# The state scan of a macaron block: the drive product written over b in PSUM, and eight products moved to GpSimd

## The chip, the cores and the metric

One core of one Trainium2 chip. The metric is the device time of one execution in microseconds (us). The kernel before takes 3356.19 us, the median of 3 runs (3346.16 to 3364.49). Engines by their names in the profile: PE is TensorE (PEld its weight loads), DVE is VectorE, ACT is ScalarE, POOL is GpSimd, SP is SyncE.

## The reference

The input x is 8 sequences of 256 tokens of width 128. Three residual parts follow each other: x + 0.5 F(norm x), then x + M(norm x), then x + 0.5 F(norm x) again, with F a stack of 6 layers of windowed attention and a gated feed-forward, 16 heads of 64. The change lies in M alone, a selective state space layer with 16 states:

```python
A = -jnp.exp(A_log)
dt = jax.nn.softplus(u @ W_dt + b_dt)
Bt = u @ W_B
Ct = u @ W_C
def step(h, inp):
    dt_t, B_t, C_t, u_t = inp
    dA = jnp.exp(dt_t[..., None] * A)
    h = dA * h + (dt_t * u_t)[..., None] * B_t[:, None, :]
    y = jnp.einsum('bdn,bn->bd', h, C_t)
    return (h, y)
...
x_ssm = _selective_scan(x_conv, A_log, D_skip, W_dt, b_dt, W_B, W_C)   # ys + u * D_skip
v = _silu(x_norm @ v1_w + v1_b)
return x_ssm * v @ w2_w + w2_b
```

## The kernel before

Channels lie on the 128 partitions, tokens along the free dimension. The 2048 tokens are 4 chunks of 512 columns (2 sequences), so every tile of M is 128 x 512 f32. PSUM has eight banks of that size: seven `general` banks and `sums`.

M runs between the two stacks of attention layers. For each chunk `c` it is prepared in 24 small stages (`("prepare", c, i)`: layer norms, projections, convolution, step size), then scanned in 16 states (`("state", c, i)`), then finished in 3 stages (`("finish", c, i)`: skip term and gate, output projection, residual). That makes 64 states, numbered `at` = 16 c + i. One state is, on each engine:

- PE: `tensor_part` spreads row i of B over all partitions into `b_bank[at % 2]` (L1354, one fp32r matmul) and row i of C into `c_bank[at % 2]` (the same line), then adds the product of three states earlier into the accumulator bank (`pe_added`, L1406, an fp32 matmul with the identity that the profile records as two).
- ACT: `act_decay` makes exp(dt A) two states ahead (L1548); a copy brings c from PSUM to SBUF as `c_kept` (L1568).
- DVE: `dve_drive` multiplies `m_dtu` (dt times u) by b out of PSUM into an SBUF tile `drive[at % 3]` (L1417), one state ahead; `tensor_tensor_scan` runs h = decay h + drive over the 512 columns (L1433), both inputs and the output in SBUF.
- POOL: `gpsimd_part` multiplies h by c into `hc` (L1622).

Two more products belong to the change: at prepare stage 23 DVE makes `m_dtu = m_dt * m_u` (L1537), and at finish stage 0 DVE adds the skip term to the accumulated y (L1439) and multiplies it by the gate (L1443). Each occurs once per chunk.

The order is fixed when the program is built. `parts_beside` gives each engine a list of parts: three states in each of the last six steps of the first attention stack (18 states), and the other 46 states behind that stack. After each state at most two side stages (prepare, finish, start) follow. A side stage stands after the state of its own slot on DVE and POOL, one state later on ACT and two states later on PE (`SIDE_LATE`). Every engine works through its list in order, and waits on semaphores.

The waits around b: PE may fill `b_bank[at % 2]` again when `m_drive` says that drive `at - 2` is done. PE may fill `c_bank` when `c_kept` of `at - 2` is done. DVE issues drive `at + 1` ahead of scan `at`.

Of the kernel before, what the change touches and what calls it, by code (L numbers as in the profile page):

```python
# [28 lines left out]
STATES = 16  # L29
# [349 lines left out]
def macaron_kernel(nc, x_in, consts_in, vec_in, mvec_in, wqkv_in, wo_in, w1_in, w2_in,  # L379
                   mw_in, wb_in, out):  # L380
    ctx = ExitStack()
    with ctx:
# [73 lines left out]
        m_xn, m_centered, m_square, m_turned = ([prep_tiles[c % 3][j] for c in range(CHUNKS)] for j in range(4))  # L456
        m_z, m_e, m_ln, m_corr = m_xn, m_centered, m_square, m_turned
        m_u, m_dt, m_dtu, m_gate = ([(v_tiles[4:8] + tiles)[4 * c + j] for c in range(CHUNKS)] for j in range(4))
        decay, hc, c_kept, hstate, drive, m_y = tiles[12:16], tiles[16:20], tiles[20:23], tiles[23:26], tiles[26:29], v_tiles[0:2]
        bc = [wqkv_hi[:, 2:, :].rearrange("p a c -> p (a c)")[:, c * COLS:(c + 1) * COLS] for c in range(CHUNKS)]  # L460
        b_bank, c_bank, acc_bank = general[2:4], general[4:6], [general[6], sums]

# [878 lines left out]
        def tensor_part(e, w, kind, c, i):  # L1341
            if kind == "state":
                at = c * STATES + i
                if at == 0:

                    for sem, value in BANKS.before_states:
                        w.wait_ge(S[sem], value)
                    w.wait_ge(S["sums_kept"], ITEMS)
                    w.wait_ge(S["m_sel"], 1)
                w.wait_ge(S["m_bc_parts"], c + 1)  # L1350
                for row, g, done, read in ((i, b_bank, "m_b", "m_drive"), (STATES + i, c_bank, "m_c", "m_c_kept")):
                    w.wait_ge(S[read], at - 1)
                    sel = row_sel[:, row:row + 1].broadcast_to([P, P])
                    e.matmul(g[at % 2][:, :], sel, bc[c], start=True, stop=True).then_inc(S[done], 1)  # L1354
                if at >= 3:
                    pe_added(e, w, at - 3)
            elif kind == "added":
                pe_added(e, w, c * STATES + i)
            elif kind == "finish":
                if i == 1:  # L1360
                    w.wait_ge(S["m_gated"], c + 1)
                    g = pe_bank(w, ("m_last", c))
                    e.matmul(g[:, :], mw[:, 3, :], m_y[c % 2], start=True, stop=True).then_inc(S["m_last"], 1)
            elif kind == "start":
                if i == 0:
                    pe_enter(e, w, 1, 0, 0)
                elif i == 2:
                    pe_enter(e, w, 1, 0, 1)
            elif kind == "out":
                w.wait_ge(S["half_added"], CHUNKS + i + 1)  # L1370
                g = pe_bank(w, ("out", i))
                for j in range(4):
                    turn = e.transpose(g[:, j * P:(j + 1) * P], x[:, (4 * i + j) * P:(4 * i + j + 1) * P], ident)
                turn.then_inc(S["out_turned"], 1)
            elif kind == "prepare":
                if i == 0:
                    w.wait_ge(S["half_added"], c + 1)
                    g = pe_bank(w, ("m_center", c, 0))
                    e.matmul(g[:, :], center, chunk(c), start=True, stop=True).then_inc(S["m_centered0"], 1)
                elif i == 7:  # L1380
                    w.wait_ge(S["m_scaled0"], c + 1)
                    g = pe_bank(w, ("m_center", c, 1))
                    e.matmul(g[:, :], center, m_xn[c], start=True, stop=True).then_inc(S["m_centered1"], 1)
                elif i in (2, 9):
                    w.wait_ge(S[f"m_squared{i // 7}"], c + 1)
                    g = pe_bank(w, ("m_var", c, i // 7))
                    e.matmul(g[:, :], mean, m_square[c], start=True, stop=True).then_inc(S[f"m_var{i // 7}"], 1)
                elif i == 14:
                    w.wait_ge(S["m_affine"], c + 1)
                    w.wait_ge(S["m_loaded"], 48)  # L1390
                    for name, m in (("m_x1", 0), ("m_v1", 1)):
                        g = pe_bank(w, (name, c))
                        e.matmul(g[:, :], mw[:, m, :], m_xn[c], start=True, stop=True).then_inc(S[name], 1)
                elif i == 18:
                    w.wait_ge(S["m_u"], c + 1)
                    g = pe_bank(w, ("m_dt", c))
                    e.matmul(g[:, :], mw[:, 2, :], m_u[c], start=True, stop=True).then_inc(S["m_dt"], 1)
                    g = pe_bank(w, ("m_bc", c))
                    e.matmul(g[:, :], wbc, m_u[c], start=True, stop=True).then_inc(S["m_bc"], 1)
# [12 lines left out]
        def dve_drive(e, w, at):  # L1412
            c = at // STATES
            w.wait_ge(S["m_b"], at + 1)
            w.wait_ge(S["m_drive_in"], c + 1)
            w.wait_ge(S["m_scan"], at - 2)
            e.tensor_tensor(drive[at % 3], m_dtu[c], b_bank[at % 2][:, :], ALU.mult).then_inc(S["m_drive"], 1)  # L1417

        def vector_part(e, w, kind, c, i):
            r = c % 2  # L1420
            if kind == "state":
                at = c * STATES + i
                if at == 0:
                    scan_tiles_free(w)
                    w.wait_ge(S["m_ahead_zeroed"], 1)
                    dve_drive(e, w, 0)
                if at + 1 < CHUNKS * STATES:
                    dve_drive(e, w, at + 1)
                w.wait_ge(S["m_drive"], at + 1)
                w.wait_ge(S["m_decay"], at + 1)  # L1430
                w.wait_ge(S["m_hc"], at - 2)

                e.tensor_tensor_scan(hstate[at % 3], decay[at % 4], drive[at % 3], 0.0, ALU.mult, ALU.add).then_inc(S["m_scan"], 1)  # L1433
            elif kind == "finish":
                if i == 0:
                    w.wait_ge(S["m_acc"], (c + 1) * STATES)
                    w.wait_ge(S["m_last"], c - 1)
                    w.wait_ge(S["m_step"], 2)
                    e.scalar_tensor_tensor(out=m_y[r], in0=m_u[c], scalar=mcol(M_D), in1=acc_bank[r][:, :], op0=ALU.mult, op1=ALU.add)\  # L1439
                        .then_inc(S["m_skip"], 1)  # L1440
                    w.wait_ge(S["m_skip"], c + 1)
                    w.wait_ge(S["m_gate"], c + 1)
                    e.tensor_tensor(m_y[r], m_y[r], m_gate[c], ALU.mult).then_inc(S["m_gated"], 1)  # L1443
                elif i == 2:
                    w.wait_ge(S["m_last"], c + 1)
                    e.scalar_tensor_tensor(out=chunk(c), in0=general_of(("m_last", c))[:, :], scalar=mcol(M_W2B), in1=chunk(c),
                                           op0=ALU.add, op1=ALU.add).then_inc(S["m_done"], 1)
            elif kind == "start":
                if i == 3:
                    dve_enter(e, w, 1, 0, 1)  # L1450
                elif i == 5:
                    dve_enter(e, w, 1, 0, 2)
                elif i == 7:
                    dve_first_splits(e, w, 1)
            elif kind == "half":

                w.wait_ge(S[f"base{i}_loaded"], 16 * (c + 1))
                w.wait_ge(S["ffn_added"], c * ITEMS + ITEMS - CHUNKS + i + 1)
                e.scalar_tensor_tensor(out=chunk(i), in0=chunk(i), scalar=0.5, in1=base[i], op0=ALU.mult, op1=ALU.add)\
                    .then_inc(S["half_added"], 1)  # L1460
            elif kind == "out":
                w.wait_ge(S["out_turned"], i + 1)

                w.wait_ge(S["valued"], (2 * ITEMS - 1) * GROUPS)
                e.tensor_copy(stage_out[:, 4 * i:4 * i + 4, :], general_of(("out", i)).rearrange("p (h d) -> p h d", d=P))\
                    .then_inc(S["out_kept"], 1)
            elif kind == "prepare":
                dve_prepare(e, w, c, i)

        def dve_prepare(e, w, c, i):  # L1470
# [57 lines left out]
            elif i == 23:  # L1528
# [4 lines left out]
                e.tensor_tensor(m_ln[c], m_ln[c], m_corr[c], ALU.subtract).then_inc(S["m_ln1"], 1)  # L1533
                w.wait_ge(S["m_ln1"], c + 1)
                e.scalar_tensor_tensor(out=m_dt[c], in0=m_z[c], scalar=0.0, in1=m_ln[c], op0=ALU.max, op1=ALU.add).then_inc(S["m_step"], 1)
                w.wait_ge(S["m_step"], c + 1)
                e.tensor_tensor(m_dtu[c], m_dt[c], m_u[c], ALU.mult).then_inc(S["m_drive_in"], 1)  # L1537

        def vector_scan(e, w):
            for what in SCAN_ORDER["DVE"]:  # L1540
# [66 lines left out]
        def gpsimd_part(e, w, kind, c, i):  # L1607
# [15 lines left out]
            elif kind == "start":  # L1623
                if i == 1:
                    pool_enter(e, w, 1, 0, 0)
                elif i == 5:
                    pool_enter(e, w, 1, 0, 2)
            elif kind == "prepare":
                if i in (1, 8):
                    w.wait_ge(S[f"m_kept{i // 7}"], c + 1)  # L1630
# [4 lines left out]
                elif i == 13:  # L1635
                    w.wait_ge(S["m_back1"], c + 1)
                    e.tensor_tensor(m_centered[c], m_centered[c], m_square[c], ALU.mult).then_inc(S["m_scaled1"], 1)
                    w.wait_ge(S["m_scaled1"], c + 1)
                    e.tensor_scalar(m_xn[c], m_centered[c], mcol(M_G), mcol(M_B), ALU.mult, ALU.add).then_inc(S["m_affine"], 1)

        def gpsimd_scan(e, w):
            for what in SCAN_ORDER["POOL"]:
# [94 lines left out]
```

## Time and profile before

| | before |
|---|---|
| median of 3 runs | 3356.19 us |
| profiled execution, its own time | 3364.97 us |
| its span, first to last instruction | 3363.2 us |
| busy: PE / DVE / POOL / ACT | 86% / 87% / 72% / 61% |
| granted TensorE clock, mean | 0.946 |
| M's scan, first drive to end of last scan | 1584.46 to 1793.14 us, 208.7 us |

In the page's forty slices of the span (84 us each) the scan fills slices 19 to 21, between the two attention stacks; there PE and POOL are less busy than elsewhere and DVE is not. In a group of instructions the columns are: line, engine, operation, output<-inputs, shape, count, then busy us and mean ns of one, then the idle time of the engine just ahead of the group and what ended it. In a timeline the columns are the start in us, the duration in us, engine, line and operation; brackets hold the idle time before it. An SBUF tile is named by the buffer in which it lies: the `hstate` and `drive` tiles are `v_buf`; the decay tiles are `q_ring` or `k_ring`; a bank of PSUM is `general` or `sums`.

### The profile page before, as it was taken

Reading aid. Unit: us, or ns where it says so; the run is one execution under the profiler, and the core shown is the slowest. Engines: PE = TensorE matmul, PEld = TensorE weight load, DVE = VectorE, ACT = ScalarE, POOL = GpSimd, SP = SyncE. Lnnn points to the kernel's source line nnn. Section 1 sums busy time; section 2 is a strip of 40 time slices with the busy share of each in tenths; the row PEclk is TensorE's granted clock in tenths of the full one; section 3 lists DMA queues with packets and bytes.
Section 4 is the critical chain, followed back from the end, with each engine's and each line's share of the span. In section 5 each row is a group of like instructions: output and inputs, shape, how many; then the busy total and the mean of one; then the engine's idle time right before and its main releaser. Section 6 shows DMA issues by size and latency. Waiting matters only on the chain. (4 is left out here: it accounts for less than half of the span.)

```text
span 3363.2 us, 132089 instructions
## 1 busy us (share of the span) xinstructions
PE 2891.1 (86%) x57914; PEld 1829.9 (54%) x57914; DVE 2933.3 (87%) x4224; ACT 2059.8 (61%) x3820; POOL 2423.5 (72%) x1679
## 2 busy tenths in 40 slices
PE   5689988988999989897677788999998989998987
PEld 3455555655666655553233455555565555555553
DVE  6789989999999988986898789889899989898984
ACT  3466666666676666665663566666566666566663
POOL 3678787787787787874464678778787787787773
PEclk8899999999999999998897899999999999999998
DMA  5233333333333333320002233333343333342330
GB/s 136 65 80 77 82 91 74 84 92 71 84 92 73 89 85 72 88 65 28 10 4 59 68 81 78 75 93 77 73 101 73 86 90 71 82 94 65 88 74 15
DMA packets 114726, 250.85 MB, mean 75 GB/s; under 512 B 27244, under 2 KB 60648, under 8 KB 114152
## 3 DMA queue, kind: packets, MB, share of 16 engines
q1 hardware_dynamic: 114152, 242.40, 30.5%
q8 instruction: 457, 7.49, 1.0%
q14 instruction: 117, 0.96, 0.1%
HBM read 37.82 MB, written 3.15 MB: 12 GB/s over the span
## 5 line engine op out<-in xcount | busy, mean ns | idle before, releaser
L1096 ACT ACTIVATE squares<-general 128x512 f32<-128x512 f32 x768 | 453.7, 597 | 716.8 <-PE general L661 707.8
L1290 POOL TENSOR_TENSOR probs<-probs,row_sum 128x1024 f32<-128x1024 f32 x192 | 365.4, 1903 | 442.4 <-DVE row_sum L968 442.3
L1270 POOL TENSOR_TENSOR q_ring<-q_ring,partner 128x512 f32<-128x512 f32 x384 | 491.0, 1279 | 203.9 <-DMA partner<-sines 203.3
L881 DVE TENSOR_TENSOR sines<-general,layer_tables 128x512 f32<-128x512 f32 x768 | 515.8, 672 | 85.3 <-ACT squares L1096 81.8
L1270 POOL TENSOR_TENSOR k_ring<-k_ring,partner 128x512 f32<-128x512 f32 x384 | 490.9, 1278 | 0.0
L695 PE MATMUL general<-probs_t,v_buf 32*64 32x64 f32 x24576 | 339.0, 234 | 153.8 <-issue 85.1
L659 PE MATMUL general<-xs_hi,wqkv_lo 128*128 128x512 f32 x768 | 454.2, 591 | 18.5 <-DVE xs_lo L908 8.0
L695 PEld LDWEIGHTS general<-probs_t,v_buf 32*64 32x64 f32 x24576 | 304.0, 134 | 246.1 <-issue 237.5
L1284 POOL TENSOR_TENSOR probs<-probs,q_scale 128x1024 f32<-128x1024 f32 x192 | 365.4, 1903 | 15.1
L722 PE MATMUL general<-k_ring,q_ring 64*32 64x64 f32 (+1 forms) x24576 | 295.3, 223 | 92.5 <-issue 53.1
L671 PE MATMUL general<-att,wo 128*128 128x512 f32 x768 | 366.2, 621 | 4.6 <-ACT att L1166 4.2
L1276 POOL TENSOR_TENSOR probs<-probs,row_max 128x1024 f32<-128x1024 f32 x192 | 366.7, 1910 | 0.0
L722 PEld LDWEIGHTS general<-k_ring,q_ring 64*32 64x32 f32 x24576 | 261.1, 105 | 126.8 <-issue 109.4
L661 PE MATMUL general<-xs_hi,wqkv_hi 128*128 128x512 f32 x768 | 313.1, 408 | 2.3 <-issue 2.2
L660 PE MATMUL general<-xs_lo,wqkv_hi 128*128 128x512 f32 x768 | 313.1, 408 | 1.9 <-issue 1.9
L659 PEld LDWEIGHTS general<-xs_hi,wqkv_lo 128*128 128x128 f32 x768 | 152.1, 198 | 267.9 <-issue 235.5
L1166 ACT ACTIVATE att<-general 128x256 f32<-128x256 f32 x768 | 231.4, 388 | 93.0 <-PE general L695 92.6
L902 DVE STREAM_TRANSPOSE v_buf<-general 128x512 f32<-128x512 f32 x384 | 264.8, 690 | 25.4 <-PE general L754 25.2
L733 PE MATMUL sums<-squares,consts 128*32 128x512 f32 x1536 | 249.0, 612 | 38.8 <-ACT squares L1096 36.5
L963 DVE TENSOR_REDUCE row_sum<-probs 128x16 f32<-128x1024 f32 x192 | 230.2, 1199 | 52.2 <-ACT probs L1173 51.8
L951 DVE TENSOR_TENSOR probs<-general,k_inv 128x512 f32<-128x512 f32 x384 | 244.8, 677 | 29.7 <-PE general L722 27.7
L752 PE MATMUL general<-xs_hi,wqkv_lo 128*128 128x256 f32 x768 | 258.7, 337 | 3.5 <-issue 3.5
(233 smaller groups left out, 6369.9 us busy)
## 6 DMA issues: line engine op xcount, KB each, us to landing
partner<-sines SPq DMA_DIRECT2D x1536, 128.0 KB, 2.3
wqkv_raw<-in_wqkv SPq DMA_DIRECT2D x80, 208.0 KB, 2.7
wo<-in_wo SPq DMA_DIRECT2D x12, 512.0 KB, 5.1
w<-in_w SPq DMA_DIRECT2D x12, 341.0 KB, 3.2
base_dram<-x SPq DMA_DIRECT2D x8, 256.0 KB, 2.4
att<-in_wqkv SPq DMA_DIRECT2D x2, 1024.0 KB, 6.7
sines<-base_dram SPq DMA_DIRECT2D x8, 256.0 KB, 3.9
w<-in_w SPq DMA_DIRECT2D x12, 128.0 KB
```

The costliest lines, as they stand in the source:

```text
L659: e.matmul(g[:, :], wqkv_lo[:, p, cut], xs_hi[:, r, :], start=True, stop=False)
L660: e.matmul(g[:, :], wqkv_hi[:, p, cut], xs_lo[:, r, :], start=False, stop=False)
L661: e.matmul(g[:, :], wqkv_hi[:, p, cut], xs_hi[:, r, :], start=False, stop=True)\
L671: done = e.matmul(g[:, :], wo[:, p, :], att[:, p, :], start=(p == OUT_PAIRS[i][0]), stop=(p == OUT_PAIRS[i][-1]))
L695: done = e.matmul(o, lhs, rhs, start=(kb == 0), stop=True, skip_group_check=True)
L722: done = e.matmul(o, qw, kw, start=False, stop=True, skip_group_check=True)
L881: e.tensor_tensor(by_seq(sines[:, i % 2, which, :]), g, both(layer_tables[:, 2 * which + 1, :]), ALU.mult).then_inc(S[f"sin_{side}"], 1)
L1096: e.activation(squares[:, (2 * p + which) % 4, :], general_of(("proj", k, n, p, which))[:, :], ACT.Square).then_inc(S[f"squared_{side}"], 1)
L1270: e.tensor_tensor(y, y, partner[:, i % 2, which, :], ALU.add).then_inc(S[f"rotated_{side}"], 1)
L1276: e.tensor_tensor(y, y, spread_keys(row_max[:, i % 2, :]), ALU.subtract).then_inc(S["max_off"], 1)
L1284: e.tensor_tensor(y, y, spread_keys(q_scale8[:, n % 2, group, :]), ALU.mult).then_inc(S["q_norms_off"], 1)
L1290: e.tensor_tensor(y, y, spread_keys(row_sum[:, i % 2, :]), ALU.mult).then_inc(S["probs_done"], 1)
```

## The change

The drive is written back over b, in the bank from which b is read, and the scan takes it from there; the three SBUF tiles for it are gone. The drive of a state is now issued just ahead of its own scan. PE may fill a bank of b again when the scan that read it is done. The `m_dtu` product and the gate product go from DVE to POOL, at the same slots.

```diff
-        decay, hc, c_kept, hstate, drive, m_y = ..., tiles[26:29], v_tiles[0:2]
+        decay, hc, c_kept, hstate, m_y = ..., v_tiles[0:2]
...
-                for row, g, done, read in ((i, b_bank, "m_b", "m_drive"), (STATES + i, c_bank, "m_c", "m_c_kept")):
+                for row, g, done, read in ((i, b_bank, "m_b", "m_scan"), (STATES + i, c_bank, "m_c", "m_c_kept")):
                     w.wait_ge(S[read], at - 1)
...
             w.wait_ge(S["m_b"], at + 1)
             w.wait_ge(S["m_drive_in"], c + 1)
-            w.wait_ge(S["m_scan"], at - 2)
-            e.tensor_tensor(drive[at % 3], m_dtu[c], b_bank[at % 2][:, :], ALU.mult).then_inc(S["m_drive"], 1)
+            b = b_bank[at % 2][:, :]
+            e.tensor_tensor(b, b, m_dtu[c], ALU.mult).then_inc(S["m_drive"], 1)
...
-                    dve_drive(e, w, 0)
-                if at + 1 < CHUNKS * STATES:
-                    dve_drive(e, w, at + 1)
+                dve_drive(e, w, at)
                 w.wait_ge(S["m_drive"], at + 1)
                 w.wait_ge(S["m_decay"], at + 1)
                 w.wait_ge(S["m_hc"], at - 2)
-                e.tensor_tensor_scan(hstate[at % 3], decay[at % 4], drive[at % 3], 0.0, ALU.mult, ALU.add).then_inc(S["m_scan"], 1)
+                e.tensor_tensor_scan(hstate[at % 3], decay[at % 4], b_bank[at % 2][:, :], 0.0, ALU.mult, ALU.add).then_inc(S["m_scan"], 1)
...   in vector_part, finish 0, and in dve_prepare, stage 23: removed; in gpsimd_part, the same stages: added
+            elif kind == "finish":
+                if i == 0:
+                    w.wait_ge(S["m_skip"], c + 1)
+                    w.wait_ge(S["m_gate"], c + 1)
+                    e.tensor_tensor(m_y[c % 2], m_y[c % 2], m_gate[c], ALU.mult).then_inc(S["m_gated"], 1)
...
+                elif i == 23:
+                    w.wait_ge(S["m_step"], c + 1)
+                    e.tensor_tensor(m_dtu[c], m_dt[c], m_u[c], ALU.mult).then_inc(S["m_drive_in"], 1)
```

## Rows read from the trace of the kernel before

**Rows 1.** Busy time by engine in the scan, granted clock, DMA share.
```profile
core 0: us, PE busy (x) PEld busy (x) DVE busy (x) ACT busy (x) POOL busy (x), PEclk, DMA share, GB/s
1584.40:1793.20 208.80, 147.09 (x317) 64.48 (x315) 194.71 (x208) 134.58 (x193) 110.40 (x78) 0.86 0.02 7
```

**Rows 2.** All waits of DVE in the scan: us in total, times, longest.
```profile
DVE v_buf L1417 <- PE general L1354: 9.8, 6, 2.6
DVE squares L1488 <- PE general L1387: 1.1, 1, 1.1
DVE partner L1502 <- PE general L1393: 1.1, 1, 1.1
DVE att L1485 <- PE general L1383: 0.3, 1, 0.3
DVE v_buf L1433 <- ACT q_ring L1548: 0.2, 1, 0.2
DVE att L1488 <- PE general L1387: 0.2, 1, 0.2
```

**Rows 3.** Groups of DVE instructions in the scan, by line and operands.
```profile
L1433 DVE TENSOR_TENSOR_SCAN v_buf<-k_ring,v_buf 128x512 f32<-128x512 f32 x32 | 51.3, 1602 | 0.0
L1433 DVE TENSOR_TENSOR_SCAN v_buf<-q_ring,v_buf 128x512 f32<-128x512 f32 x32 | 49.6, 1549 | 0.2 <-ACT q_ring L1548 0.2
L1417 DVE TENSOR_TENSOR v_buf<-q_ring,general 128x512 f32<-128x512 f32 x48 | 31.8, 662 | 3.6 <-PE general L1354 3.5
L1443 DVE TENSOR_TENSOR v_buf<-v_buf,k_ring 128x512 f32<-128x512 f32 x2 | 2.2, 1109 | 0.1
L1443 DVE TENSOR_TENSOR v_buf<-v_buf 128x512 f32<-128x512 f32 x1 | 1.6, 1576 | 0.0
L1537 DVE TENSOR_TENSOR q_ring<-k_ring,q_ring 128x512 f32<-128x512 f32 x3 | 2.5, 842 | 0.1
```

**Rows 4.** Minimum, median, maximum ns of L1417 (one input in PSUM) and L1433.
```profile
L1417 DVE TENSOR_TENSOR v_buf<-q_ring,general x48: 627/657/689, 1647.9 to 1789.5; 128x512 f32<-128x512 f32 x48
L1433 DVE TENSOR_TENSOR_SCAN v_buf<-q_ring,v_buf x32: 1209/1388/1989, 1586.0 to 1790.1; 128x512 f32<-128x512 f32 x32
```

**Rows 5.** Timeline of DVE and POOL in two states, 1652 to 1657.
```profile
1653.08 1.22 DVE L1433 TENSOR_TENSOR_SCAN v_buf<-q_ring,v_buf 128x512 f32<-128x512 f32 x1
1654.21 0.66 DVE L1417 TENSOR_TENSOR v_buf<-q_ring,general 128x512 f32<-128x512 f32 x1
1654.43 1.27 POOL L1622 TENSOR_TENSOR q_ring<-v_buf,k_ring 128x512 f32<-128x512 f32 x1 [3.20 <-DVE v_buf L1433]
1654.79 1.98 DVE L1433 TENSOR_TENSOR_SCAN v_buf<-k_ring,v_buf 128x512 f32<-128x512 f32 x1
1656.70 0.66 DVE L1417 TENSOR_TENSOR v_buf<-q_ring,general 128x512 f32<-128x512 f32 x1
```

**Rows 6.** Timeline of a DVE pair in which the second reads the first's output.
```profile
1674.92 0.69 DVE L1533 TENSOR_TENSOR att<-att 128x512 f32<-128x512 f32 x1
1675.65 0.69 DVE L1535 SCALAR_TENSOR_TENSOR k_ring<-att 128x512 f32<-128x512 f32 x1
```

**Rows 7.** ACT instructions that write PSUM, groups of 1560 to 1900.
```profile
L1148 ACT ACTIVATE general<-mask_bf 128x512 f32<-128x512 bf16 x7 | 3.9, 590 | 0.0
```

**Rows 8.** Timeline of PE, one state at the full clock, one at half.
```profile
1658.03 1.03 PE L1354 MATMUL general<-wqkv_hi,row_sel 128*128 128x512 f32 x2
1659.36 1.03 PE L1354 MATMUL general<-wqkv_hi,row_sel 128*128 128x512 f32 x2
...
1605.54 1.84 PE L1354 MATMUL general<-wqkv_hi,row_sel 128*128 128x512 f32 x2
1608.10 1.84 PE L1354 MATMUL general<-wqkv_hi,row_sel 128*128 128x512 f32 x2
```

**Rows 9.** Timeline of the end of the scan, from the last two products on POOL.
```profile
1791.95 1.19 DVE L1433 TENSOR_TENSOR_SCAN v_buf<-k_ring,v_buf 128x512 f32<-128x512 f32 x1
1792.16 2.04 POOL L1622 TENSOR_TENSOR q_ring<-v_buf 128x512 f32<-128x512 f32 x1 [1.21 <-DVE v_buf L1433]
1794.16 1.26 POOL L1622 TENSOR_TENSOR k_ring<-v_buf,q_ring 128x512 f32<-128x512 f32 x1
1798.68 0.69 DVE L1443 TENSOR_TENSOR v_buf<-v_buf,k_ring 128x512 f32<-128x512 f32 x1
1799.42 1.12 PE L1363 MATMUL general<-v_buf,wqkv_raw 128*128 128x512 f32 x2 [1.57 <-DVE v_buf L1443]
1800.59 0.75 DVE L1446 SCALAR_TENSOR_TENSOR x<-general,mvec,x 128x512 f32<-128x512 f32 x1 [1.22 <-PE general L1363]
```

More of the change, by code:

```diff
@@ L458, in macaron_kernel @@
         m_u, m_dt, m_dtu, m_gate = ([(v_tiles[4:8] + tiles)[4 * c + j] for c in range(CHUNKS)] for j in range(4))
-        decay, hc, c_kept, hstate, drive, m_y = tiles[12:16], tiles[16:20], tiles[20:23], tiles[23:26], tiles[26:29], v_tiles[0:2]
+        decay, hc, c_kept, hstate, m_y = tiles[12:16], tiles[16:20], tiles[20:23], tiles[23:26], v_tiles[0:2]
         bc = [wqkv_hi[:, 2:, :].rearrange("p a c -> p (a c)")[:, c * COLS:(c + 1) * COLS] for c in range(CHUNKS)]
@@ L1440, in vector_part @@
                         .then_inc(S["m_skip"], 1)
-                    w.wait_ge(S["m_skip"], c + 1)
-                    w.wait_ge(S["m_gate"], c + 1)
-                    e.tensor_tensor(m_y[r], m_y[r], m_gate[c], ALU.mult).then_inc(S["m_gated"], 1)
                 elif i == 2:
@@ L1535, in dve_prepare @@
                 e.scalar_tensor_tensor(out=m_dt[c], in0=m_z[c], scalar=0.0, in1=m_ln[c], op0=ALU.max, op1=ALU.add).then_inc(S["m_step"], 1)
-                w.wait_ge(S["m_step"], c + 1)
-                e.tensor_tensor(m_dtu[c], m_dt[c], m_u[c], ALU.mult).then_inc(S["m_drive_in"], 1)
         def vector_scan(e, w):
```

## The prediction, made before the changed kernel ran

> **What bounds the kernel now.** The page's forty slices come first: they show where M lies, and that the two attention stacks around it hold none of the changed instructions. Only the scan, 208.7 us, can gain or lose. The view of busy time by engine then shows DVE busy 194.7 of 208.8 us there, PE 147, ACT 135, POOL 110 [rows 1]. The list of DVE's waits adds the rest: 9.8 + 1.1 + 1.1 + 0.3 + 0.2 + 0.2 = 12.7 us of idle, 12.5 of it ended by PE [rows 2]. So DVE sets the pace and PE is next. The granted clock is 0.86; with two levels that means about 28% of the stretch at 1.2 GHz [rows 1]. A whole state of PE's own work (b, c, one addition) goes round in 1659.36 - 1658.03 = 1.33 us at 2.4 GHz and in 1608.10 - 1605.54 = 2.56 us at 1.2 GHz [rows 8].
>
> **The scan itself.** The groups give 32 scans of 1602 ns and 32 of 1549, a mean of 1.576 us [rows 3], but the shortest take 1.21 and the longest 1.99 [rows 4]. The timeline says why: a scan with POOL idle takes 1.22. The next is called at 1654.79 while POOL's product runs from 1654.43 to 1655.70, and ends at 1656.77, 1.07 us after POOL is done [rows 5]. The scan waits for POOL's instruction and then runs. The drive, issued in the middle of the same POOL instruction, takes 0.66, and all 48 of its group lie between 0.627 and 0.689 [rows 4]: a DVE instruction with one input in PSUM isn't held. In the change the scan has one SBUF input and one in PSUM, as the drive has. I take it as unheld: 1.21 us.
>
> **Part 1, the states.** Before, start to start: drive to scan 0.58 (1654.21 to 1654.79), scan to next drive its duration less 0.07 [rows 5]. Per state 0.58 + 1.576 - 0.07 = 2.09 us, and 64 of them 133.5 us. After, the scan needs the drive just issued. A dependent pair on DVE starts 1675.65 - 1674.92 = 0.73 us apart for a first of 0.69, that is 0.04 after its end, where independent ones overlap by 0.07 [rows 6, 5]. The drive of 0.66 gives 0.70 to the scan, the scan 1.21 - 0.07 = 1.14. Per state 1.84 us, 64 of them 117.8: **15.7 us less**, of which the held time is 64 x 0.366 = 23.4 and the new dependence takes back 64 x 0.12 = 7.7.
>
> No row has DVE writing PSUM or waiting on its own write there. Bounds of that write: ACT writes a bank in 0.590 us [rows 7], no slower than DVE's 0.66, so nothing at the low end. At the high end reading and writing one bank could run at the pace of the scan, 1.21 for 512 columns: 0.55 more per state, 35 us. The dependence through PSUM may cost 0 to 0.3 us per state instead of 0.12: 8 us better to 12 worse. The scan's read from PSUM: the drive (PSUM and SBUF) has 0.657 as median, the pair of SBUF inputs 0.69 [rows 4, 6], so 0.03 to either side, 2 us. I take the values from the nearest rows, that is no surcharge for PSUM.
>
> The Trainium skill speaks against this: "VectorE: DVE Perf Modes", section on the TRN2 errata, gives a VectorE instruction from PSUM a fixed 120 cycles and one from SBUF 58, at 0.96 GHz 0.065 us more, an estimate of 4 us for 64 scans. The trace has the PSUM reader no slower (0.657 against 0.69) [rows 4, 6], so the sum goes without it.
>
> **Part 2, the products.** DVE loses 4 gate products and 4 of dt with u. In the scan that is 2 x 1.109 + 1.576 + 3 x 0.842 = 6.3 us [rows 3], less about 0.03 overlap each; the first chunk's product of dt and u stands just ahead of the scan and its 0.6 us comes off the start. Together **6.5 us less** on DVE, and some gaps behind them. POOL gets eight instructions of 1.27 [rows 5]. It has 98 us idle in the scan [rows 1] and needs 1.27 of a 1.84 us state. Behind each new wait on POOL (for the skip term, for the step) stands the next `hc`; its scan is queued on DVE behind the same step, so `hc` isn't late, and only `pe_added` three states later reads it. `m_dtu` is made at least three states before its chunk begins. Cover for eight instructions: all but the last gate. There the path is open: 1.27 plus a handover of 0.13 (1654.30 to 1654.43) in place of 0.69 costs 0.7 us [rows 5, 9]. Against it the `hc` of state 62 is no longer held (2.04 becomes 1.27), which returns 0.8 [rows 9]. The end costs nothing.
>
> **Part 3, what loses its cover.** PE fills b of state at+2 when scan `at` is done, before when drive `at` was, an instruction pair and more earlier. In a bare state this is harmless: b comes some 0.6 us after scan `at`, an estimate from the handover to PE of 0.05 [rows 9] and half of the 1.03 that the two spreads take [rows 8]; DVE wants it 1.84 us after. It isn't harmless where PE has a side stage for DVE. Such a stage stands behind state s+1 in PE's list, its reader behind state s on DVE. PE now starts that state at the end of scan s-1, hears of it after 0.05, needs 1.33 us for the state [rows 8] and 1.12 for an fp32 pair [rows 9], 2.5 us in all at the full clock; DVE arrives after 1.84. That is a stall of 0.66 us where DVE has no side stage in the slot before, and at half clock, with twice 1.12 for the pair, 2.56 + 2.24 - 1.84 = 3.0. Before, PE had 5.9 us for it (three scans, two drives), and such waits sum to 2.7 us [rows 2]. I count 16 such handovers in the order (stages 2, 7, 9, 14, 18 of chunks 1 to 3, where they lie in the scan, three finishes, one start). Seven tenths of them uncovered: 11 x (0.72 x 0.66 + 0.28 x 3.0) = **14 us more** as the high end, 5 if the clock stays up, nothing if other side stages hide them. At half clock PE's 2.56 us also cuts the gain of bare states. Since PE would idle less, I take a clock a little better than now, and **11 us** for all of part 3.
>
> **Sum.** 15.7 + 6.5 - 11 = 11 us less. Against the profiled execution's own time (3364.97; the span 3363.2 and 1.8 us around it) that is 3354. This execution lies 8.8 us above the median of the runs, so the forecast against the median is 3356 - 11 = **3345 us**. What follows the scan waits for it, the last finish stage leads straight into the second stack [rows 9], so the gain isn't given back behind.
>
> **Rivals.**
> A, the cover holds: DVE's other side work hides PE's handovers, part 3 is 1 us. Gain 21, 3335. For it: DVE has 194.7 - 64 x 2.24 = 51 us of side instructions between states [rows 1, 3], which give PE time. Against: the stages of one chunk alternate between the engines, and the slot before a reader has mostly no DVE work.
> B, slower: PE becomes the bound by its handovers. Place: the first matmul of a side stage behind state s+1, which now waits for scan s-1. At 1.2 GHz a stall of 3.0 at all 16 is 48 us against the gain of 22: 26 slower, 3382; it decides from a mean stall of 22/16 = 1.4 us. For it: the clock already stands at 0.86. Against: 72% of the stretch is at the full clock, where it costs 0.66. With half of them at the low clock it is 16 x 1.8 = 29, 7 slower: 3363.
> C, the drive over its own bank runs at half pace: +35 - 22 + some waits of part 3 hidden: 3369 us.
> D, the change doesn't do what it says: the scan is held by POOL as before. Then the dependence stays as a cost: +7.7 - 6.5, and 4 of part 3: 3361. Against: all 64 drives.
>
> **How the numbers follow.** About 0.5% (17 us) is what a measurement of this kernel can tell from no change. Forecast (3341 to 3351) 0.46; A 0.30; B 0.12; C 0.05; D 0.07. Faster by over 0.5% means below 3339: most of A and a little of the forecast, 0.32. Slower by over 0.5%, over 3373: half of C and the upper part of B, 0.06. The rest, 0.62, is the same. The range for 8 in 10 reaches from A's far side with the clock up (3331) to D and the mild form of B (3363).
>
> **What would show it.** L1433 at 1.2 us with hardly a spread, and POOL's L1622 at 1.27 throughout; the drive's group still 0.66 with `general` as output; 0.7 us from drive to scan. The scan shorter by 11 us, to about 198. DVE's waits for PE at L1485, L1488, L1502 and L1517 grown from 2.7 us towards 12, with some for L1446. The forecast is wrong if the drive takes over 0.8 us, if scans stay near 1.6, or if these waits stay below 4 or pass 20 us.

## The result

| | before | changed |
|---|---|---|
| median of 22 runs each | 3364.71 us (3346.16 to 3387.69) | 3343.80 us (3321.07 to 3365.50) |
| ratio | | 0.9932, 95% interval 0.9914 to 0.9949 |
| M's scan in the profiled execution | 208.7 us | 191.2 us |
| span of the profiled execution | 3363.2 us | 3319.3 us |

The changed kernel is 0.68% faster, 23 us of 3364.71 (17 to 29 by the interval). The forecast was 11 us faster with a chance of 0.32 for more than 17. The forecast time, 3345, lies 1 us beside the measured 3343.8 by luck of the reference: the median of before stood at 3356 in three runs and stands at 3365 in 22. What must be judged is the gain, and by the whole times it is about twice what was forecast.

### The profile page after: what moved, and what is told of

It is laid out like the page before. It is cut to its first block and busy times, and to the rows that moved or that the text cites. A ratio compares the mean times of both kernels' runs of the same rounds, so it can differ in the third digit from the quotient of the medians.

```text
span 3319.3 us, 132032 instructions
## 1 busy us (share of the span) xinstructions
PE 2881.9 (87%) x57914; PEld 1834.8 (55%) x57914; DVE 2903.0 (87%) x4216; ACT 2061.6 (62%) x3820; POOL 2419.8 (73%) x1687
```

## The profile after

Busy time by engine in three stretches: ahead of the scan, the scan (first drive to end of last scan, the answer to [rows 1]), behind it.

```profile
0.00:1571.00 1571.00, 1370.98 (x28804) 884.00 (x28805) 1376.82 (x2026) 969.78 (x1825) 1162.67 (x811) 0.95 0.34 82
1571.00:1762.10 191.10, 141.35 (x318) 64.99 (x317) 168.11 (x202) 136.61 (x193) 104.90 (x84) 0.88 0.02 7
1762.10:3319.30 1557.20, 1369.56 (x28795) 885.83 (x28793) 1358.09 (x1990) 955.23 (x1802) 1152.24 (x792) 0.95 0.33 78
```

DVE's busy time in the scan falls by 26.6 us (194.7 to 168.1), and the scan by 17.5; the 9 us between are new idle time. This execution also shows the two attention stacks 13 us shorter each than the profile before (1584.5 and 1570). The changed instructions aren't there; the experiments below show that these two numbers scatter and that the scan's doesn't.

The groups on DVE that answer to [rows 3], then the spread of the scan [rows 4]:

```profile
L1431 DVE TENSOR_TENSOR_SCAN v_buf<-q_ring,general 128x512 f32<-128x512 f32 x32 | 39.1, 1221 | 2.5 <-ACT q_ring L1541 1.5
L1417 DVE TENSOR_TENSOR general<-general,q_ring 128x512 f32<-128x512 f32 x48 | 32.7, 681 | 0.1
...
L1431 DVE TENSOR_TENSOR_SCAN v_buf<-q_ring,general x32: 1220/1221/1222, 1573.1 to 1759.1; 128x512 f32<-128x512 f32 x32
```

The scan's spread is gone: 1.220 to 1.222 us in all 64, where it was 1.19 to 2.21. Two states of the timeline, the answer to [rows 5]:

```profile
1755.36 1.22 DVE L1431 TENSOR_TENSOR_SCAN v_buf<-q_ring,general 128x512 f32<-128x512 f32 x1
1756.50 0.68 DVE L1417 TENSOR_TENSOR general<-general,q_ring 128x512 f32<-128x512 f32 x1
1756.72 1.28 POOL L1615 TENSOR_TENSOR q_ring<-v_buf,q_ring 128x512 f32<-128x512 f32 x1 [0.57 <-PE sums L1406]
1757.21 1.22 DVE L1431 TENSOR_TENSOR_SCAN v_buf<-k_ring,general 128x512 f32<-128x512 f32 x1
```

POOL's product now covers the first 0.8 us of the scan at 1757.21 and neither is held. A state is 1757.21 - 1755.36 = 1.85 us (2.09 as the mean before). All waits of DVE in the scan, the answer to [rows 2], come to 20.6 us (12.7 before). The list has the wait just ahead of the first drive, 0.8 us here and 0.4 before, which stands outside the stretch; inside it they are 19.7 and 12.3:

```profile
DVE att L1483 <- PE general L1387: 3.1, 2, 2.5
DVE att L1480 <- PE general L1383: 2.7, 1, 2.7
DVE att L1512 <- PE general L1397: 2.0, 1, 2.0
DVE partner L1497 <- PE general L1393: 1.8, 2, 1.4
DVE general L1417 <- PE general L1354: 1.8, 1, 1.8
DVE x L1441 <- PE general L1363: 1.5, 2, 0.8
DVE v_buf L1431 <- ACT q_ring L1541: 1.5, 1, 1.5
DVE squares L1512 <- PE general L1397: 1.4, 1, 1.4
DVE squares L1483 <- PE general L1387: 1.4, 2, 0.7
DVE norm_t L847 <- PE general L642: 1.2, 1, 1.2
DVE general L1417 <- POOL k_ring L1610: 0.8, 1, 0.8
DVE v_buf L1512 <- PE general L1397: 0.7, 1, 0.7
DVE squares L1480 <- PE general L1383: 0.7, 1, 0.7
```

Waits of DVE for results of PE's side stages are 16.5 us, 2.7 before. The wait of the drive for b is 1.8, 9.8 before. One handover in the timeline, at the full clock:

```profile
1662.24 0.74 PE L1354 MATMUL general<-wqkv_hi,row_sel 128*128 128x512 f32 x2 [0.86 <-DVE v_buf L1431]
1662.81 1.22 DVE L1431 TENSOR_TENSOR_SCAN v_buf<-k_ring,general 128x512 f32<-128x512 f32 x1
1662.81 1.02 PE L1406 MATMUL sums<-k_ring,consts 128*128 128x512 f32 x2
1663.67 1.02 PE L1387 MATMUL general<-squares,consts 128*128 128x512 f32 x2
1664.73 0.69 DVE L1483 TENSOR_SCALAR squares<-general 128x512 f32<-128x512 f32 x1 [0.70 <-PE general L1387]
```

PE starts b at 1662.24, when the scan before (1660.96 to 1662.18) has ended, does c and the addition, and only then the side stage; DVE stands still for 0.70 us. Last the end of the scan, the answer to [rows 9]:

```profile
1760.90 1.22 DVE L1431 TENSOR_TENSOR_SCAN v_buf<-k_ring,general 128x512 f32<-128x512 f32 x1
1764.74 0.75 DVE L1437 SCALAR_TENSOR_TENSOR v_buf<-q_ring,mvec,sums 128x512 f32<-128x512 f32 x1 [2.61 <-PE sums L1406]
1765.56 1.26 POOL L1625 TENSOR_TENSOR v_buf<-v_buf,k_ring 128x512 f32<-128x512 f32 x1 [2.05 <-DVE v_buf L1437]
1768.36 0.75 DVE L1441 SCALAR_TENSOR_TENSOR x<-general,mvec,x 128x512 f32<-128x512 f32 x1 [2.88 <-PE general L1363]
```

Before, the skip term stood here:

```profile
1797.89 0.75 DVE L1439 SCALAR_TENSOR_TENSOR v_buf<-q_ring,mvec,sums 128x512 f32<-128x512 f32 x1 [4.75 <-PE sums L1406]
```

From the end of the last scan to the start of the last residual it is 1768.36 - 1762.12 = 6.2 us, 1800.59 - 1793.14 = 7.5 before, 1.2 us less. The gate on POOL isn't free there: from the skip term to the residual it is 1768.36 - 1764.74 = 3.6 us, 1800.59 - 1797.89 = 2.7 before, 0.9 more. The gain lies ahead of the skip term. POOL's last `hc` ends 1.4 us after the last scan (2.3 before), which returns the 0.9. From there to the skip term it is 1.2 us (2.5 before), because PE's last additions ran at a granted clock of 1.00 (1762 to 1766) and before at 0.62 (1793 to 1799; 0.63 in the second profile of before).

## The experiments

Ratios are against the kernel before on the same chip, with their 95% interval; the interval is about 0.2% to each side, 7 us. The length of the scan (first drive to end of last scan) comes from one profile of each and is the finer measure, as the second profiles show. The rows below each are of the view of busy time by engine, for the scan.

**The kernel before again.** No edit. 

> The kernel before once more, for a second profile: the scan 208.7 us within 2 us, while the attention stacks ahead of it and behind it (1584.5 and 1570.0 us in the first) move by 5 us and more. Rival (the stacks repeat as the scan does, so the 13 us that each was shorter in the first profile of the changed kernel come from the change): 1584 and 1570 within 2 us.

```profile
0.00:1584.10 1584.10, 1375.43 (x28803) 884.32 (x28804) 1375.42 (x2026) 970.66 (x1826) 1161.16 (x810) 0.95 0.34 81
1584.10:1792.90 208.80, 147.73 (x317) 64.94 (x315) 194.61 (x208) 134.55 (x193) 110.33 (x78) 0.86 0.02 7
1792.90:3359.30 1566.40, 1375.37 (x28795) 889.05 (x28795) 1355.99 (x1990) 954.77 (x1802) 1152.22 (x792) 0.94 0.33 77
```

Measured 3361.14 us. The scan repeats within 0.1 us and its waits one by one. The stacks moved little here, 0.4 and 3.6 us, less than the 5 us that I expected.

**The changed kernel again.** No edit. 

> The changed kernel once more, for a second profile of it on the chip of the other three. The theory: the scan 191 us again within 3 us (17 us shorter than 208.7), while the two attention stacks, 13 us shorter each in the first profile of the changed kernel, scatter; ratio 0.993. Rival (the stacks gain too): the stacks are again 1571 and 1557 us, 13 us less each than in the profile before.

```profile
0.00:1590.60 1590.60, 1380.16 (x28797) 888.02 (x28804) 1380.47 (x2026) 969.75 (x1825) 1162.05 (x811) 0.95 0.34 81
1590.60:1780.80 190.20, 137.06 (x318) 63.06 (x317) 168.12 (x202) 136.23 (x193) 104.99 (x84) 0.91 0.02 7
1780.80:3348.40 1567.60, 1373.15 (x28789) 885.53 (x28793) 1359.86 (x1990) 954.33 (x1802) 1151.82 (x792) 0.95 0.33 77
```

Ratio 0.9944 (0.9921 to 0.9967), medians 3339.50 against 3359.17. The scan is 190.2 us, 1 less than in the first profile; the stacks are 1590.6 and 1567.6, that is 20 and 10 longer than in the first profile of the same kernel. Over all profiles of this study the part ahead of the scan lies between 1567 and 1597 us. So the 13 us that each stack seemed to gain is scatter, and the gain of the change is 18 us in the scan and 1.2 at its end, 19 to 20. That lies in both intervals (11 to 27 and 17 to 29 us).

**The products alone.** The kernel before with only the moves to POOL:

```diff
 (vector_part, finish 0)      -  e.tensor_tensor(m_y[r], m_y[r], m_gate[c], ALU.mult)...
 (dve_prepare, stage 23)      -  e.tensor_tensor(m_dtu[c], m_dt[c], m_u[c], ALU.mult)...
 (gpsimd_part, same stages)   +  both
```

> The kernel before with only the eight products moved to GpSimd; the drive stays an SBUF tile made one state ahead. The theory (the scan bound by VectorE, terms add up): the scan is 6 us shorter than the 208.7 us of before, scans still held by GpSimd at about 1.58 us mean, ratio near 0.998. Rival (the terms do not add, most of the gain needs a free VectorE): within 2 us of before, because the time goes into more held scans. A second rival: more than 10 us, if the products were worth more than their own length because of the gaps behind them.

```profile
1596.30:1807.20 210.90, 146.34 (x317) 63.81 (x315) 191.37 (x202) 134.87 (x193) 119.54 (x84) 0.86 0.02 7
...
L1433 DVE TENSOR_TENSOR_SCAN v_buf<-k_ring,v_buf 128x512 f32<-128x512 f32 x32 | 53.1, 1661 | 0.0
L1433 DVE TENSOR_TENSOR_SCAN v_buf<-q_ring,v_buf 128x512 f32<-128x512 f32 x32 | 51.0, 1595 | 0.8 <-ACT q_ring L1543 0.8
...
DVE partner L1499 <- PE general L1393: 5.5, 2, 2.7
```

Ratio 1.0015 (0.9995 to 1.0034), the scan 2.2 us longer. The theory is out and the rival is nearer, though not by its reason alone: 6.3 us of work left DVE and only 3.2 came back as longer scans (104.1 against 100.9 us of them), 6.1 as waits. Of the new waits 4.4 are for PE's matmul of stage 14 (L1393: 5.5 us against 1.1). In one of the two PE itself stood 5.3 us for POOL's part of stage 13 (L1639), 1.7 before, and the moved product (L1642, at 1650.12) ran on POOL just ahead of that part. POOL's busy time in the scan rose from 110.4 to 119.5: each product moved there is one more instruction that a held scan, or POOL's own side stages, may have to wait for.

**The scan from PSUM alone.** The changed kernel with both products back on DVE. 

> The change with the eight products back on VectorE: the drive is written over b and read there. The theory: scans at 1.22 us without spread, 64 x 0.24 = 15 us of states less, minus some 8 us of new waits for TensorE, plus 4 us of side operations that are held less: the scan 11 us shorter than before, ratio near 0.997. Rival (the fewer held side operations come from the moved products): side operations as before, the scan 7 us shorter.

```profile
1566.90:1765.60 198.70, 142.52 (x318) 66.36 (x317) 174.75 (x208) 135.78 (x193) 98.45 (x78) 0.87 0.02 7
```

Ratio 0.9965 (0.9942 to 0.9987), the scan 10.0 us shorter, 11 expected. The rival is out: DVE's side operations without the products take 54.2 us, as in the changed kernel (54.0) and less than before (57.3), so it is not the moved products that free them. The products are then worth another 7.5 to 8.5 us (198.7 to 191.2 and 190.2), where alone they were worth nothing. The two halves of the change don't add: 10 and -2.2 alone, 17.5 to 18.5 together.

**GpSimd's product made short**, in the kernel before:

```diff
-  e.tensor_tensor(hc[at % 4], hstate[at % 3], c_kept[at % 3], ALU.mult)
+  e.tensor_tensor(hc[at % 4][:, 0:32], hstate[at % 3][:, 0:32], c_kept[at % 3][:, 0:32], ALU.mult)
```

> The kernel before with GpSimd's product of h and c made over 32 of the 512 columns only (the rest of hc is left as it was, so part of the computation is left out). The theory (scans are held by that GpSimd instruction): scans at 1.21 us nearly all, 23 us off 208.7, the scan 186 us or, where TensorE's low clock then binds, 190. Rival (the spread of the scans has another cause, such as the writes of ScalarE): scans still 1.5 us and more, the scan over 203 us.

```profile
1585.90:1766.60 180.70, 139.84 (x317) 62.21 (x315) 166.26 (x208) 133.09 (x193) 36.03 (x78) 0.89 0.02 8
...
L1433 DVE TENSOR_TENSOR_SCAN v_buf<-k_ring,v_buf x32: 1191/1218/2195, 1589.8 to 1765.4; 128x512 f32<-128x512 f32 x32
```

Ratio 0.9905 (0.9878 to 0.9931). The scans fall to a median of 1.22 with the drive still in SBUF, and the stretch to 180.7 us: POOL's instruction is what held them. The 28 us are 5 more than the 23 I expected, and made up differently: the scans give 17.5 (their mean is 1.30, as a few still take 2.2; POOL's other instructions are as long as before), and DVE's side operations, freed too, give 10.5.

**The same in the changed kernel.** 

> The changed kernel with GpSimd's product of h and c over 32 of the 512 columns (the rest of hc is left out). The theory (in the changed kernel GpSimd's product no longer holds the scan, only side operations with two SBUF inputs): scans 1.22 us as before, some 4 to 6 us of held side operations go, the scan 185 to 188 us against 190.6. Rival (GpSimd still paces the loop through hc, the addition and the banks): the scan 175 us or less.

```profile
1584.90:1768.60 183.70, 136.89 (x319) 62.06 (x317) 162.05 (x202) 136.32 (x193) 40.41 (x84) 0.91 0.02 8
```

Ratio 0.9916 (0.9889 to 0.9944). The scans stay at 1.220 to 1.222, and 6.5 to 7.5 us go, a little more than expected: DVE's busy time falls by 6.1. So what POOL's `hc` still costs in the changed kernel are the side operations that it holds, not the scans.

**The order alone.** The kernel before, with the drive of a state issued just ahead of its own scan, still into SBUF:

```diff
-                    dve_drive(e, w, 0)
-                if at + 1 < CHUNKS * STATES:
-                    dve_drive(e, w, at + 1)
+                dve_drive(e, w, at)
```

> The kernel before with one edit: the drive of a state is issued just ahead of its own scan, still into SBUF. The theory that the scan waits for GpSimd's product until 1.4 us after the scan before has ended, while the dependent drive is done after 0.63: the dependence costs nothing here, the scan stays within 2 us of 208.7. Rival (the dependence costs its 0.12 us in every state whatever holds the scan): 8 us longer, 216 us.

```profile
L1431 DVE TENSOR_TENSOR_SCAN v_buf<-k_ring,v_buf x32: 1223/1596/2323, 1595.1 to 1797.4; 128x512 f32<-128x512 f32 x32
```

Ratio 0.9976 (0.9956 to 0.9996), the scan 208.2 us. The scans are still held, so it is the input in PSUM that frees them and not the order. From drive to scan it is 0.70 us here too, 0.58 before, yet the total doesn't grow: the scans are 3 us shorter in sum, so part of the dependence hides behind the hold, and DVE's waits are 4.2 us shorter (8.5 against 12.7), at a granted clock of 0.88 against 0.86.

**Order and short product.** 

> The kernel before with both edits: the drive issued just ahead of its own scan (into SBUF), and GpSimd's product of h and c over 32 of the 512 columns (the rest of hc is left out). Beside the short product alone (scan 180.7 us) this shows what the dependence costs where nothing holds the scan. The theory: drive to scan 0.70 us start to start in place of 0.58, 64 x 0.12 = 8 us onto 180.7, to 188, with fewer waits for b perhaps 185. Rival (the dependence is free): 181 or less.

 Ratio 0.9923 (0.9896 to 0.9949), the scan 180.8 us against 180.7 with the short product alone. My number missed: nothing is added in total. The dependence is there, and what it took came back elsewhere: from drive to scan it is 0.70 us against 0.58, DVE's busy time is 169.9 us against 166.3 (its instructions overlap less), its waits are 7.8 us against 13.4, and the granted clock is 0.92 against 0.89. That PE used the small delay per state to catch up fits these numbers, but no run shows it apart from the clock.

**The drive ahead again.** The changed kernel with the drive of the next state issued ahead of the scan (the order of before), over b in its two banks. 

> The changed kernel with the drive of the next state again issued ahead of the scan, still written over b in its two banks. The b of that state can be filled only when the scan before the one just issued is done, so VectorE waits for TensorE's b in every state: about 0.6 us at the full clock and 1 us at the low one. The theory (b comes 0.6 us after the scan that frees its bank): 64 x 0.6 = 38 us and more onto the scan, 191 to about 230 us, slower than before by some 20 us, waits of the drive for L1354 near 40 us. Rival (the dependence of the scan on the drive just issued is the larger cost, and issuing ahead hides it): the scan shorter than 191.

```profile
1589.80:1789.00 199.20, 141.00 (x317) 61.69 (x315) 168.02 (x202) 137.26 (x193) 104.83 (x84) 0.90 0.02 7
...
DVE general L1417 <- PE general L1354: 26.0, 35, 3.2
```

Ratio 0.9965 (0.9947 to 0.9983), the scan 8 to 9 us longer than in the changed kernel. The waits for b are there, 26 us in 35 states, about 0.6 where nothing lies between; in the other states a side operation covers them, and the waits for side stages nearly vanish (1.6 us): having stood at the drive, DVE comes later to them (argued from the order, not tested apart). I expected 38 and left out that one wait displaces the other. With the drive over b, issuing it just ahead of its own scan is worth 8 to 9 us.

**PE's side stages one state late everywhere.** The changed kernel with

```diff
-SIDE_LATE = {"PE": 2, "DVE": 0, "ACT": 1, "POOL": 0}
+SIDE_LATE = {"PE": 1, "DVE": 0, "ACT": 1, "POOL": 0}
```

> The changed kernel with the side stages of TensorE one state behind VectorE's list instead of two (SIDE_LATE PE 1). The theory (TensorE's side stages now start behind a state that waits for the scan before, and so come 0.7 us or more late for VectorE): with one state less the waits of VectorE for L1387, L1383, L1397, L1393 and L1363 (about 14 us in the scan after the change) fall to under 5, the scan is 6 to 10 us shorter than 191, ratio to before near 0.990. Rival (the order was not the cause, the waits are for the slow clock or for GpSimd and ScalarE, and TensorE is now blocked by its own inputs): the waits move to the b of the drive (L1417) and the scan is as long or longer.

```profile
DVE x L991 <- PE general L774: 4.6, 1, 4.6
DVE general L1417 <- PE general L1354: 3.4, 3, 2.7
```

Ratio 0.9944 (0.9919 to 0.9970), the scan 189.3 us, 1 to 2 shorter where 6 to 10 were expected. Behind the attention the waits for side stages did go (0.6 us left, some 8 in the changed kernel), but beside the attention PE now stood at its side stages and came late with the feed-forward (the row of L991) and with b.

**One state late only behind the attention.** The changed kernel, PE's lag 2 in the first 18 states and 1 after:

```diff
-            at += slots.get(s - late, [])
+            if engine != "PE" or s < len(host):
+                at += slots.get(s - late, [])
+            elif s == len(host):
+                at += slots.get(s - 2, []) + slots.get(s - 1, [])
+            else:
+                at += slots.get(s - 1, [])
```

> The changed kernel; TensorE's side stages stay two states behind in the first 18 states, beside the attention, and are one state behind in the 46 states after them. The theory: the waits of 0.7 to 1.4 us for L1383, L1387, L1397, L1363 in the last 46 states (some 8 us) go, and those that one state less everywhere brought beside the attention (L991 4.6 us, the drive 2.7 us) do not come: the scan 184 us against 191. Rival (the waits are only moved to the next b, as the fixed work of TensorE stays): 189 to 192.

```profile
1583.90:1770.10 186.20, 138.59 (x318) 63.40 (x317) 170.18 (x202) 135.10 (x193) 105.00 (x84) 0.89 0.02 8
```

Ratio 0.9915 (0.9896 to 0.9934), median 3329.57 against 3358.98. The scan is 186.2 us, 184 expected, 4 to 5 less than in the changed kernel; DVE's waits are 13.6 us in place of 20.6. It is the fastest complete version here. By medians it beats the changed kernel by more than its scan does (0.9915 against 0.9944 and 0.9932); the intervals overlap, and only the 4 to 5 us are shown.

## Why the prediction was right and where it was not

**The mechanism** of the states was right. The scan isn't held once one input lies in PSUM: 1.22 us as forecast, 64 times. Rival D (still held) and rival C (half pace over its own bank) are out: the drive takes 0.681 us against 0.662. PSUM costs the scan nothing that shows: with its drive just ahead it takes 1.221 us from PSUM and 1.224 from SBUF (order and short product), and 1.210 from PSUM where the drive stands a scan earlier (the drive ahead again). The surcharge for PSUM that the prediction worked out from the Trainium skill ("VectorE: DVE Perf Modes", section on the TRN2 errata), 0.065 us, is not borne out here. A state takes 1.85 us, 1.84 forecast. The states save 64 x 0.24 = 15.4 us, 15.7 forecast. Of the signs given, the waits for side stages (16.5 us, wrong below 4 or above 20) and the durations came out; the stretch was to be about 198 us and is 191.

**The products** leave 6.3 us, as forecast. That they are worth this and more only with the other half of the change was not in the prediction: its sum took the parts as independent, and the run with the products alone (2.2 us longer) shows that they aren't.

**Part 3 was mis-sized.** It stood at 11 us and measured 20.6 - 12.7 = 7.9, of which 7.4 lie inside the stretch (19.7 - 12.3). The handovers were forecast at 0.66 us each and measure 0.70 in the timeline; the waits for side stages rose by 13.8 us, the high end of the 14 worked out. What I left out is that waits displace each other: the drive's waits for b, 9.8 us [rows 2], fell to 1.8, as DVE now stands at a side stage where it stood at the drive. At the start of the scan the waits are 2.1 us longer (ACT's first decay, and POOL's memset just ahead of the first drive).

**A term was missing**: side operations with operands in SBUF are held less. Comparing the groups of DVE in both profiles, the multiply-adds of stage 19 take 3 x 0.69 in place of 1.27 + 1.28 + 1.29 (1.8 us less), stage 16's first 0.46 in place of 0.78 three times (1.0), stage 23's 0.9 and 0.7 less, one operation of stage 21 0.7 more: 3.7 us less. The other side operations are 0.4 us longer together, so 3.3 in all.

The tally closes: -15.4 - 6.3 + 7.4 - 3.3 = -17.6, and the scan measures 191.2 - 208.7 = -17.5. From the forecast of 11 the gain grew by 3.6 (part 3) and 3.3 (side operations), with 1.2 behind the last scan, which I had put at nothing. There the two terms of the prediction were about right and cancelled (the gate on POOL costs 0.9, 0.7 forecast; the freed `hc` returns 0.9, 0.8 forecast); the 1.2 came from the clock of PE's last additions, which no term had, and why the clock stood higher there is not shown. That makes 19; the medians say 21 and the ratio 23, with an interval that begins at 17. The rest, up to 4 us, is within what the runs can't tell.

**The rivals.** A (the cover holds, gain 21) comes closest in its number, but not in its mechanism: the cover did not hold. It had the right size because two other terms made up for it. B didn't reach its threshold: over the 16 handovers that the prediction counted the mean stall is 16.5 / 16 = 1.0 us, under the 1.4 from which it would decide. D's price was wrong as well: it charged 7.7 us for the dependence and credited 6.5 for the products, but with the scans still held the dependence alone adds nothing (208.2 us) and the products alone return nothing (210.9 us). The clock went up a little, 0.86 to 0.88 and 0.91.

## What to carry to other kernels

Where a VectorE instruction shows two durations, look at what GpSimd runs beside it before counting its work. With one of its inputs in PSUM it ran free here, so an operand that already comes from a matmul is better left there than brought to SBUF, even if that costs a dependence between neighbours. Moving work to GpSimd was worth something only after that: while the scans were still held it came back in full. Then look at where the new order has shortened another engine's lead, and move that engine's side work one slot nearer. Here that was worth 4 to 5 us of the stretch beside the 18 of the change, and only behind the attention stack.

## What the runs showed of the hardware

- A scan of 128 x 512 f32 takes 1.21 us alone with both inputs in SBUF, waits for a running GpSimd product (1.98 us with a product that had begun 0.36 us before), and takes 1.220 to 1.222 with one input in PSUM. The Trainium skill ("SBUF — State Buffer", section on who interferes with whom) says that a VectorE instruction with at most one SBUF input and outside its two-port modes doesn't contend; these 64 agree, and the same drive in the kernel before too (0.627 to 0.689) [rows 4].
- VectorE read and wrote one bank of PSUM in place at nearly the same pace: 0.681 us for 512 columns against 0.662 with an SBUF output. The dependent scan starts 0.03 us after its end (1756.50 + 0.68 to 1757.21), about as for a pair through SBUF, 0.04 [rows 6].
- A one-input `tensor_scalar` from SBUF to SBUF can be held as well: 0.40 us free and, once in the changed kernel (stage 21, at 1649.54), 1.14 beside a GpSimd product that had begun 0.43 us before.
- Two profiles of one kernel repeated the stretch of the scan within 0.1 us (before) and 1 us (changed), while the stacks with their DMAs moved by up to 4 us in the one and by 10 and 20 in the other. A profile's stretch shows a change of this size better than the whole time does.
